# A graph network kernel, logits stage: outer products formed after the linear map, the activation step and the running maximum one round later

## The reference

```python
w = h @ rw3 + roff                       # radial weights of an edge, 224 columns
Y1 = SQ3 * rhat                          # unit vector of the edge
w1, w2, w3, w4, w5 = jnp.split(w, [C0, 2*C0, 2*C0+C1, 2*C0+2*C1], axis=1)   # C0 = 64, C1 = 32
o0a = w1 * ms
o0b = w4 * (jnp.einsum('eud,ed->eu', mv, Y1) / SQ3)
o1a = (w2 * ms)[:, :, None] * Y1[:, None, :]          # the outer products, 64 x 3
o1b = w3[:, :, None] * mv
o1c = w5[:, :, None] * (jnp.cross(mv, Y1[:, None, :]) / SQ2)
ds = jnp.concatenate([o0a, o0b], axis=1)
dv = jnp.concatenate([o1a, o1b, o1c], axis=1)         # 128 x 3
ls, lv = ds @ lin_ws + lin_bs, jnp.einsum('nud,uk->nkd', dv, lin_wv)
a = jnp.einsum('ehk,hk->eh', _smooth_leaky(alpha), alpha_dot)   # alpha: columns 0:64 of ls
amax = segment_max(a, edge_dst)
```

## Time and profile before

| what | us |
|---|---|
| median of 3 runs (range) | 9317.33 (9287.5 to 9322.78) |
| the profiled execution | 9334.97 |
| its span on the core | 9333.2 |
| logits stage: first to last scan (L1458) of 98 | 903.8 to 2386.2 |

### The profile page before, as it was taken

One profiled execution on the slowest core, in us unless ns is written; L12 is line 12 of the kernel. 1 busy time (PEld: TensorE's weight loads), 2 busy tenths in 40 slices (PEclk: granted clock), 3 DMA queues, 4 the chain that ended last, 5 costly groups with the idle time before them and its releaser, 6 DMA issues. The chain is left out here.

```text
span 9333.2 us, 186439 instructions
## 1 busy us (share of the span) xinstructions
PE 6919.9 (74%) x43168; PEld 6115.7 (66%) x43168; DVE 6350.6 (68%) x22528; ACT 4143.0 (44%) x9706; POOL 5188.6 (56%) x4620
## 2 busy tenths in 40 slices
PE   3556888888544787778899866799855559999555
PEld 2444666666444777777788766688744448999554
DVE  4555777777554888888666577666566667777677
ACT  1223444454222344444444477544355554444344
POOL 3455777777454444444455488555455544444677
PEclk8776778888555899999999999899977779999665
DMA  6764333333687333333345477545444444444455
GB/s 109 133 135 103 76 76 77 77 77 76 130 163 147 85 90 91 91 93 90 102 124 124 122 210 214 151 124 125 110 140 140 139 136 114 119 119 116 139 160 154
DMA packets 1017785, 1119.53 MB, mean 120 GB/s; under 512 B 490662, under 2 KB 678918, under 8 KB 1017312
## 3 DMA queue, kind: packets, MB, share of 16 engines
q1 hardware_dynamic: 835312, 812.90, 32.5%
q0 software_dynamic: 182144, 303.59, 14.4%
HBM read 650.50 MB, written 465.65 MB: 120 GB/s over the span
## 5 line engine op out<-in xcount | busy, mean ns | idle before, releaser
L665 POOL DMA_INDIRECT agg<-seg_rows,edge_idx x1568 | 1545.3, 986 | 891.4 <-issue 621.3
L444 POOL DMA_INDIRECT erow<-e_rows,edge_idx x1176 | 1246.3, 1060 | 1238.4 <-issue 1139.1
L714 POOL TENSOR_TENSOR stats<-stats,power 128x8 f32<-128x8 f32 (+1 forms) x588 | 757.0, 1287 | 1208.7 <-DVE stats L1030 384.4
L393 PE MATMUL banks<-w_all,xt 128*128 128x128 f32 (+1 forms) x2352 | 552.5, 372 | 609.4 <-DVE y_more L941 192.2
L479 PEld LDWEIGHTS banks<-seg,mid 128*128 128x128 f32 x7840 | 931.2, 194 | 15.6
L479 PE MATMUL banks<-seg,mid 128*128 128x128 f32 x7840 | 932.2, 277 | 0.0
L393 PEld LDWEIGHTS banks<-w_all,xt 128*128 128x128 f32 x2352 | 432.7, 249 | 699.8 <-issue 683.9
L527 ACT ACTIVATE mid_t<-banks 128x512 f32<-128x512 f32 x980 | 585.4, 597 | 315.0 <-PE banks L479 313.6
L396 PE MATMUL banks<-w_all,xt 128*128 128x128 f32 x3528 | 645.9, 334 | 0.0
L396 PEld LDWEIGHTS banks<-w_all,xt 128*128 128x128 f32 x3528 | 609.3, 250 | 0.0
L491 PE MATMUL banks<-w_all,mid_t 128*128 128x161 f32 (+1 forms) x2352 | 583.5, 330 | 2.8 <-ACT res L532 2.8
(11 more groups left out here) (267 smaller groups left out, 19003.8 us busy)
## 6 DMA issues: line engine op xcount, KB each, us to landing
x_rows<-xo SPq DMA_DIRECT2D x294, 324.0 KB
xin<-x_rows SPq DMA_DIRECT2D x294, 324.0 KB
e_rows<-ets SPq DMA_DIRECT2D x294, 322.0 KB
dst_row<-in_dst_flat SPq DMA_DIRECT2D x294, 256.0 KB
xin<-in_x SPq DMA_DIRECT2D x196, 324.0 KB, 8.8
seg_rows<-res SPq DMA_DIRECT2D x196, 322.0 KB
seg_rows<-res SPq DMA_DIRECT2D x98, 384.0 KB
seg_rows<-res SPq DMA_DIRECT2D x98, 338.0 KB
```

Source lines behind the costliest of these rows:

```text
L393: pe.matmul(flat[:, to + k * cols:to + (k + 1) * cols], of[:, k * P:(k + 1) * P], W(w_s), start=True, stop=True)
L444: pool.indirect_dma_start(erow[s.quad][:, t, 0:EROW], None, table, bass.IndirectOffsetOnAxis(idx[s.slot][:, t:t + 1], 0),).then_inc(rows_i ...
L665: pool.indirect_dma_start(agg[s.quad][:, t, 0:SUM_COLS[layer]], None, seg_rows[layer], bass.IndirectOffsetOnAxis(idx[s.slot][:, t:t + 1], ...
L714: pool.tensor_tensor(st[:, at + n:at + 2 * n], st[:, at:at + n], power[:, 0:n], ALU.pow) \
```

## The change

`message` no longer forms the 64 x 3 outer products (L369). It writes the factor `w2 * ms` (64 columns) into `mid` beside the other parts, so that `mid` is 97 + 2 x 128 columns wide, three parts instead of four. `values` multiplies part 1 (factor and the x part) by `lin_vx` and part 2 (the y and z parts) by `lin_vyz`, block diagonal weights of 64 columns each. ScalarE copies the 128 result columns into `products` instead of 96 strided ones into `gate_v`. VectorE's `leaky` gets two more operations: the mapped factor times the unit vector (`outer_v`), and the sum with the mapped vectors into the row to be stored. The unit vector has its own four buffers (`unit`). `leaky` runs one round later (t - 6), `running_max` and `logits` too (t - 7), and the loads and stores that go with them; what is stored has four buffers. `load_indices` waits for the gathers of chunk t - 4 instead of its messages.

```diff
-    "lin_s": (97, 128), "lin_v": (128, 32), "adot": (128, 64),
+    "lin_s": (97, 128), "lin_vx": (128, 64), "lin_vyz": (128, 64), "adot": (128, 64),
...
-            outer = chain.did(dve.tensor_tensor(view(0, C0), w[:, :, 64:128], es, ALU.mult).then_inc(chain.sem, 1))
+            factor = view(0, C0) if outer_to is not None else m[:, :, 97:161]
+            outer = chain.did(dve.tensor_tensor(factor, w[:, :, 64:128], es, ALU.mult).then_inc(chain.sem, 1))
...
-            dve.wait_ge(chain.sem, chain.after(outer))
-            chain.did(dve.tensor_tensor(
-                outer_to, spread(view(0, C0), 2, [P, TILES, 3, C0]),
-                spread(e1[:, :, 0:3], 3, [P, TILES, 3, C0]), ALU.mult).then_inc(chain.sem, 1))
+            if outer_to is not None:
+                dve.wait_ge(chain.sem, chain.after(outer))
+                chain.did(dve.tensor_tensor(
+                    outer_to, spread(view(0, C0), 2, [P, TILES, 3, C0]),
+                    spread(e1[:, :, 0:3], 3, [P, TILES, 3, C0]), ALU.mult).then_inc(chain.sem, 1))
...
                     def load_vectors(s):
-                        sp.wait_ge(mid_step.sem, mid_step.after((s.g - 3) * steps))
+                        sp.wait_ge(ln2_step.sem, ln2_step.after((s.g - 3) * 2))
...
                     def load_indices(s):
-                        sp.wait_ge(mid_step.sem, mid_step.after((s.g - 1) * steps))
+                        sp.wait_ge(rows_in[s.slot].sem, rows_in[s.slot].after(s.half))
+                        sp.wait_ge(rows_b_in[s.slot].sem, rows_b_in[s.slot].after(s.half))
...
                     def store_values(s):
-                        sp.wait_ge(val_sb.sem, val_sb.after(2 * s.g + 2))
+                        sp.wait_ge(leaky_step.sem, leaky_step.after((s.g + 1) * leaky_steps))
                         sp.dma_start(values_dram[bass.ds(s.g * CHUNK, CHUNK), :].rearrange("(t p) c -> p t c", p=P),
-                                     gate_v[s.slot][:]).then_inc(values_out[s.slot].sem, 16)
+                                     rows_v[s.quad][:]).then_inc(values_quad[s.quad].sem, 16)
...
-                    pipeline(sp, chunks, [(load_scalars, 0), (load_vectors, 1), (load_indices, 2), (load_penalties, 5),
-                                          (store_values, 6), (store_tops, 7)])
+                    pipeline(sp, chunks, [(load_scalars, 0), (load_vectors, 1), (load_indices, 2), (load_penalties, 6),
+                                          (store_values, 8), (store_tops, 9)])
...
                     def messages_t(s):
                         pe.wait_ge(mid_step.sem, mid_step.after((s.g + 1) * steps))
-                        for k in range(4):
-                            pe.wait_ge(agg_sb.sem, agg_sb.after(4 * s.g + k - 1))
+                        for k in range(3):
+                            pe.wait_ge(agg_sb.sem, agg_sb.after(3 * s.g + k - 1))
...
-                            cut, to = slice((2 * r + t) * P, (2 * r + t + 1) * P), 224 * t
+                            cut, to = slice((2 * r + t) * P, (2 * r + t + 1) * P), 256 * t
                             pe.matmul(psum[:, 3, to:to + 128], mid_t[0:97, 0, cut], W("lin_s"), start=True, stop=True)
-                            for i in range(3):
-                                last = pe.matmul(psum[:, 3, to + 128 + 32 * i:to + 160 + 32 * i],
-                                                 mid_t[:, 1 + i, cut], W("lin_v"), start=True, stop=True)
+                            pe.matmul(psum[:, 3, to + 128:to + 192], mid_t[:, 1, cut], W("lin_vx"), start=True, stop=True)
+                            last = pe.matmul(psum[:, 3, to + 192:to + 256], mid_t[:, 2, cut], W("lin_vyz"), start=True, stop=True)
...
                     def logits(s):
-                        pe.wait_ge(leaky_step.sem, leaky_step.after((s.g + 1) * 3))
+                        pe.wait_ge(leaky_step.sem, leaky_step.after(s.g * leaky_steps + 3))
...
-                        (r2, 3), (r1, 1), (h1, 0), (h2, 2), (logits, 6), (messages_t, 5),
+                        (r2, 3), (r1, 1), (h1, 0), (h2, 2), (logits, 7), (messages_t, 5),
...
                     def values(s, r):
                         if r == 0:
-                            act.wait_ge(values_out[s.slot].sem, values_out[s.slot].after(s.half))
-                            act.wait_ge(leaky_step.sem, leaky_step.after((s.g - 1) * 3))
+                            act.wait_ge(values_quad[s.quad].sem, values_quad[s.quad].after(s.quarter))
+                            act.wait_ge(leaky_step.sem, leaky_step.after((s.g - 1) * leaky_steps))
...
-                        act.activation(gate_v[s.slot][:, two_, 0:64], ps[:, :, 64:128], ACT.Copy)
-                        act.activation(gate_v[s.slot][:, two_, 64:].rearrange("p t (c i) -> p t i c", i=3),
-                                       ps[:, :, 128:].rearrange("p t (i c) -> p t i c", i=3), ACT.Copy) \
-                            .then_inc(val_sb.sem, 1)
+                        act.activation(rows_v[s.quad][:, two_, 0:64], ps[:, :, 64:128], ACT.Copy)
+                        act.activation(products[s.slot][:, two_, :], ps[:, :, 128:], ACT.Copy).then_inc(val_sb.sem, 1)
...
-                        (logits, 6), (messages_t, 5),
+                        (logits, 7), (messages_t, 5),
...
                     def ln2(s):
+                        dve.wait_ge(leaky_step.sem, leaky_step.after((s.g - 3) * leaky_steps))
...
                         chain.did(dve.tensor_tensor(
-                            attr[s.quad][:, :, 1:6], attr[s.quad][:, :, 1:6],
+                            unit[s.quad][:, :, 1:6], attr[s.quad][:, :, 1:6],
                             spread(stats[s.slot][:, 52:56], 2, [P, TILES, 5]), ALU.mult).then_inc(chain.sem, 1))
...
                     def leaky(s):
...
+                        of, shape = products[s.slot], [P, TILES, 3, C1]
+                        k = chain.did(dve.tensor_tensor(
+                            outer_v[:], spread(of[:, :, 0:C1], 2, shape),
+                            spread(unit[s.quad][:, :, 1:4], 3, shape), ALU.mult).then_inc(chain.sem, 1))
+                        dve.wait_ge(values_quad[s.quad].sem, values_quad[s.quad].after(s.quarter))
+                        dve.wait_ge(chain.sem, chain.after(k))
+                        chain.did(dve.tensor_tensor(
+                            rows_v[s.quad][:, :, 64:].rearrange("p t (c i) -> p t i c", i=3), outer_v[:],
+                            of[:, :, C1:].rearrange("p t (i c) -> p t i c", i=3), ALU.add).then_inc(chain.sem, 1))
...
                     pipeline(dve, chunks, [
                         (ln2, 3), (ln1, 1), (message, 4), (var1, 0), (var2, 2),
-                        (lambda s: weights(s, 0), 3), (leaky, 5), (lambda s: weights(s, 1), 3), (running_max, 6)])
+                        (lambda s: weights(s, 0), 3), (leaky, 6), (lambda s: weights(s, 1), 3), (running_max, 7)])
```

More of the change, by code:

```diff
@@ L216, in gnn_kernel @@
         stats = four("stats", [P, 96])
-        gate_v = two("gate_v", [P, TILES, D])
         fm, bm = two("fm", [HEADS, CHUNK]), two("bm", [HEADS, CHUNK])
@@ L256, in gnn_kernel @@
         pre_quad = [signal(f"pre_quad_{k}", 16, 2) for k in range(4)]
-        values_in, values_out = slots("values_in", 16), slots("values_out", 16)
+        values_quad = [signal(f"values_quad_{k}", 16, 2) for k in range(4)]
+        tops_quad = [signal(f"tops_quad_{k}", 32, 2) for k in range(4)]
         xt_mm, xt_sb = signal("xt_mm"), signal("xt_sb")
@@ L1124, in edge_logits @@
                 e_ext = two("e_ext", [P, TILES, C0 + 5 * C1], own=own)
-                mid, mid_t = two("mid", [P, TILES, 97 + 3 * P], own=own), sb("mid_t", [P, 4, CHUNK], own=own)
+                mid, mid_t = two("mid", [P, TILES, 97 + 2 * P], own=own), sb("mid_t", [P, 3, CHUNK], own=own)
+                unit = [sb(f"unit_{k}", [P, TILES, 6], own=own) for k in range(4)]
+                products, outer_v = two("products", [P, TILES, P], own=own), sb("outer_v", [P, TILES, 3, C1], own=own)
                 alpha, alpha_th = two("alpha", [P, TILES, C0], own=own), two("alpha_th", [P, TILES, C0], own=own)
                 leaky_x, lg_rows = sb("leaky_x", [P, TILES, C0], own=own), two("lg_rows", [P, TILES * HEADS], own=own)
-                pen, lg = two("pen", [HEADS, CHUNK], own=own), two("lg", [HEADS, CHUNK], own=own)
+                pen = two("pen", [HEADS, CHUNK], own=own)
+                lg, top = ([sb(f"{n}_{k}", [HEADS, CHUNK], own=own) for k in range(4)] for n in ("lg", "top"))
+                rows_v = [sb(f"rows_v_{k}", [P, TILES, D], own=own) for k in range(4)]
                 VAR, SECOND = 2 * P, 2 * P
@@ L1173, in store_tops @@
                         sp.wait_ge(logit_sb.sem, logit_sb.after(s.g + 1))
-                        for k, what in enumerate((lg, fm)):
-                            sp.dma_start(tops_dram[:, k, bass.ds(s.g * CHUNK, CHUNK)], what[s.slot][:]) \
-                                .then_inc(tops_out[s.slot].sem, 16)
```

(17 more changed lines are left out.)

50 lines of the change are left out of this document (27 added, 23 removed).

## The result

The changed kernel takes 8997.88 us (median of 4 runs, 8992.68 to 9019.54) against 9316.9 us before: a ratio of 0.967, 95% interval 0.964 to 0.969. I had forecast 9185 us and a range of 9125 to 9275; the direction held, but the saving that I forecast (132 us) was less than half of what came (319). The profiled execution took 9019.54 us, 315.5 us less than the one before.

The account below looks back on a forecast made before the run. It took the logits round (15.38 us) to be bound by TensorE and ScalarE's ring; terms of -2.3 us gave 13.1, but GpSimd held it at 14.0, saving about 132 us: 9185 us, range 9125 to 9275.

Parts of the forecast that it names:

- Every gain or loss is a length of a round times about 97, and nothing else moves.: Only the logits stage changes: a round takes 15.38 us, 98 of them 1507 us, 16% of the span.
- GpSimd next, at 14.0 us: Logits stage: GpSimd's gathers, gaps and root, 13.96 us a round, keep rounds from falling to 13.1; 14.0 taken.
- after which I expect the same stretching: `leaky`'s new run of operations would stretch GpSimd's gathers as L369 did; mean gather stays near 1.16 us.
- Less contention: Rival: with L369 gone GpSimd's logits round falls to 13.3 to 13.75 us; 9115 us at 13.3; chance 0.18.
- Part 1: Logits round: the messages' fourth part goes, with four transposes and one ScalarE copy; -0.6 us a round.
- Part 2: Matmuls of `values`: six passes of 32 columns a tile become four of 64; -1.3 us a round, bounds -1.8 to +0.8.
- Part 5: ScalarE's copies in `values`: `products`, 256 contiguous, for the strided 192; -0.1 us a round, bounds -0.2 and 0.
- Part 3: `leaky` a round later: its wait of 2.9 us goes, but the round gains 0, bounds -0.5 to 0.
- Part 6: VectorE loses L369, gains two operations of 384 elements: net +0.17 to +0.4 us, priced 0, covered by `leaky`'s lost wait.
- the ring: TensorE and ScalarE's chain in the logits round (roots, squares, `silu`, transposes, copies, `values` twice), taken as bound: 15.38 to 13.1 us.
- Part 4: SyncE: `load_indices` released earlier, so `h1` no longer waits for its load; -0.3 us a round.
- The rival of TensorE's clock: Logits stage: fewer matmuls leave TensorE idle, so its lower clock holds longer; rounds 14.3 to 15.3 us; chance 0.2.

Follow-up runs that it names:

- The pads: Idle one-column memsets behind VectorE's logits loop: kernel before with 12 or 45, third node layer 835.8 us; changed kernel with 211, 956.9 us.
- after_old_sync: Changed kernel with `load_indices` waiting for the messages of the round before again: 9045 us, 0.966-0.969 of the kernel before.
- after_pad140: Changed kernel with 140 one-column memsets behind VectorE's logits loop: 9283 us, 0.961-0.972 of the kernel before.
- factor_only: Changed kernel with `leaky`, the maxima and the stores at their old rounds: 9274 us, 0.993-0.997 of the kernel before.
- pad12: Kernel before with 12 one-column memsets behind VectorE's logits loop: 9714 us, 0.984-0.994 of the kernel before.
- pad45: Kernel before with 45 one-column memsets behind VectorE's logits loop: 9710 us, 0.984-0.994 of the kernel before.
- after_pad100: Changed kernel with 100 one-column memsets behind VectorE's logits loop: 9512 us, 0.963-0.975 of the kernel before.

## Why the prediction was right or wrong

**"Every gain or loss is a length of a round times about 97, and nothing else moves."** Wrong, and the largest error: 120 of the 184 us by which I missed. VectorE's instruction list grew by 45 ahead of the third node layer, and its loop there left a place in which it stood for 6 to 7 us in each pass, 5.5 us of them lost. The gaps stood in the trace before, in a layer that I had not opened. The pads show that the cause is the place and nothing the change computes.

**GpSimd next, at 14.0 us.** Right in kind, too long by 0.56 us a round, about 54 us. The failing step is "after which I expect the same stretching". It failed in place: over 1000 to 2000 us, 68% of the time of `leaky`'s five operations lies under GpSimd's root and 24% under gathers. It failed in size too: the 29 gathers that did start under L1456, its last operation, took 1.13 us in the mean, where the 53 that started under L369 before took 1.57. A stretch of the changed kernel's timeline shows the place:

```profile
1526.82 2.31 POOL L1207 TENSOR_TENSOR stats<-stats,power 128x12 f32<-128x12 f32 x1
1526.95 0.42 DVE L1443 SCALAR_TENSOR_TENSOR leaky_x<-alpha_th,alpha 128x256 f32<-128x256 f32 x1
...
1528.78 0.68 DVE L1456 TENSOR_TENSOR rows_v<-outer_v,products 128x384 f32<-128x384 f32 x1
1529.31 1.01 POOL L1200 DMA_INDIRECT work<-src_table,edge_idx  x1 [0.18 <-issue]
```

The root is a little longer for it (2.38 us in the mean, 2.30 before), the gathers went from 1.16 to 1.08 us. Eight times 0.08 is 0.64 us; putting the outer product back restores 8 x (1.135 - 1.082) = 0.42 of it, or 0.34 by the 1.093 of after_old_sync. "Less contention", which I gave 0.18, was what happened, with a mean gather (1.08) between the one that it named (1.05) and mine, and at 13.4 us of its 13.3 to 13.75. Its reason, that one of two stretchers goes, was right; its doubt, that `leaky` puts its run beside gathers, was the part that did not come. On chip C, in after_pad140, it did: there 21% of that run lies under the root and 61% under gathers.

**Part 1**, -0.6: not measured by itself. **Part 2**, -1.3: the four passes of one tile take, in the changed kernel's timeline, 0.95 us at the lower clock and 0.56 at the upper:

```profile
1509.36 0.53 PE L1298 MATMUL banks<-w_all,mid_t 128*128 128x64 f32 x2
...
1509.68 0.63 PE L1299 MATMUL banks<-w_all,mid_t 128*128 128x64 f32 x2
...
1524.34 0.33 PE L1298 MATMUL banks<-w_all,mid_t 128*128 128x64 f32 x2
...
1524.51 0.39 PE L1299 MATMUL banks<-w_all,mid_t 128*128 128x64 f32 x2
```

(from the first start to the last end), against 1.33 and 0.75: -0.8 a round at the upper clock and -1.5 at the lower, where I had -1.0 and -1.8. **Part 5**: the copy of `products` is 405 ns, my straight line gave 384.

**Parts 3 and 6**, 0 each: wrong as separate terms. Part 3 alone came to 33 us, 0.34 a round, within its bounds. Part 6 is near nothing only if part 3 is made too. With `leaky` at its old place VectorE's two operations (1.24 us) are in the ring and factor_only is 114 us slower in its stage; I had named the cover ("the wait that it loses") and priced its loss at 39 us, and it cost about 300. The operations' own time is 1.24 x 97 = 120 us of that; the rest came with the lower clock, and how isn't settled. The strided addition, 681 ns, is within the 0.56 to 0.78 that I gave.

**Part 4**, -0.3: -0.2 at most within the change, and no gain alone.

**The rival of TensorE's clock** did not come for the whole change: 0.87 was granted where it had been 0.82. It came for factor_only (0.62), and there it ate all of the gain. The mechanism that it named, fewer matmuls and so more idle time for TensorE, is not shown: the changed kernel has the same 60 matmuls a round and the higher clock, and TensorE in factor_only is busy for 86% of the time, more than the 84% before. On chips B and C the changed kernel's round was 15.8 to 16.8 us at 0.74 to 0.77, with GpSimd waiting 2.3 to 3.3 us a round: there this rival describes the stage better than GpSimd's round does, and the ratio is still 0.96 to 0.98. On B the kernel before has rounds of 18.8 and 19.2 us (pad12 and pad45), so it suffers more; on C it has no trace.

after_pad100, after_pad140 and the changed kernel can't be told apart by their ratios; nothing that computes the whole was faster than the changed kernel beyond the intervals.

## What to carry to other kernels

Before pricing an edit, look for gaps that an engine spends on nothing in every pass of a loop anywhere in the program: adding or removing instructions ahead of that loop can make or remove them, and here that was worth 1.3%, more than a third of the result; a control with a dozen idle instructions behind the changed stage showed it in one run. Two edits that share an engine's slack have one price together, so test the halves before crediting either. And when a contention partner is removed, the bound's figure has to be worked out anew by what will then run beside it.

## What the runs showed of the hardware

- A loop of 268 VectorE instructions stood for 6 to 7 us in each pass at starts 3164 and 3420 and cost 5.5 us a pass more than at ten other starts, with 110 packets more on the instruction queue.
- Chips differ: the same kernel took 9317 us on one and 9854 on another, at a mean clock of 0.83 against 0.80; the logits round was 15.4 us on the first, and 18.8 and 19.2 for the kernel with 12 and 45 memsets behind that stage on the second.
- The granted clock can settle: 0.60 in round after round of factor_only, with 60 matmuls a round, where the changed kernel had 0.87 with as many and the kernel before 0.82 with 72.
- A gather that starts under a product of two inputs and 768 elements (0.95 us) takes 1.57 us; one that starts under a sum over 768 elements of one input (0.94 us, 12 elements written) takes 0.95, as it does alone.
